# Adding the input rows on GpSimd instead of VectorE in the last stage of an attention and mixture-of-experts layer

## The reference

```python
x = x + _layernorm(_L0_attn_ref(_layernorm(x, axis=-1), ...), axis=-1)
x = x + _layernorm(_L0_ffn_ref(_layernorm(x, axis=-1), ...), axis=-1)
return x

def _L0_ffn_ref(hidden_states, ...):
    ...
    routed_sum = routed.sum(axis=0)
    shared = jax.nn.silu(x @ shared_gate_w) * (x @ shared_up_w) @ shared_down_w
    return (shared + routed_sum).reshape(orig_shape)
```

## Time and profile before

| | us |
|---|---|
| median of 3 runs | 421.2 (420.75 to 421.65) |
| the profiled execution, its time | 420.75 |
| the profiled execution, its span | 418.9 |
| PE busy in the span | 397.9 (95%) |
| DVE busy in the span | 274.7 (66%) |
| POOL busy in the span | 122.9 (29%) |

### The profile page before, as it was taken

The page is one execution under the profiler, slowest core; times in us unless marked ns, Lnnn a source line. Parts: engine busy times, 40 slices in busy tenths (PEclk is TensorE's granted clock), DMA queues, the critical chain, the costliest instruction groups (busy, mean ns, idle before and its releaser), DMA issues.

```text
span 418.9 us, 9551 instructions
## 1 busy us (share of the span) xinstructions
PE 397.9 (95%) x3443; PEld 301.6 (72%) x3443; DVE 274.7 (66%) x644; ACT 207.1 (49%) x381; POOL 122.9 (29%) x179
## 2 busy tenths in 40 slices
PE   8998999999999999898989999999999999999992
PEld 8775557676767766575768999999995444489991
DVE  5565677987879777877674694222225898736786
ACT  2745748586776757556551113444447766411110
POOL 2424514335152525303402002211222220015651
PEclk9999999999999999999999999999999999999998
DMA  8735235373634636360146750011111111114532
GB/s 259 220 109 151 64 84 189 92 228 89 217 90 123 193 87 211 101 196 1 55 140 204 246 189 27 27 50 52 52 50 39 52 40 39 40 47 120 152 113 75
DMA packets 50772, 47.29 MB, mean 113 GB/s; under 512 B 5350, under 2 KB 45542, under 8 KB 50726
## 3 DMA queue, kind: packets, MB, share of 16 engines
q1 hardware_dynamic: 44795, 38.31, 30.7%
q0 software_dynamic: 1632, 4.46, 3.7%
q10 hardware_dynamic: 4299, 3.92, 2.8%
HBM read 25.19 MB, written 8.65 MB: 81 GB/s over the span
## 4 chain that ended last, share of the span: by engine, by line
PE 81%; DVE 9%; issue 3%; ACT 3%; POOL 2%; DVEq 0%; ACTq 0%; POOLq 0%
PE bank L1420 41%; PE bank L1752 7%; PE bank L1424 6%; PE bank L1597 6%; PE bank L1617 5%; PE bank L1558 4%; PE bank L1777 3%; DVE nmax L1087 2%; PE bank L1496 2%; PE bank L1544 2%; PE bank L1433 2%; PE bank L1486 1%; DVE wall L1117 1%; DVE stats_at L991 1%; POOL rstd_at L644 1%
## 5 line engine op out<-in xcount | busy, mean ns | idle before, releaser
L1087 DVE TENSOR_REDUCE nmax<-bank 128x2 f32<-128x512 f32 x112 | 74.3, 686 | 27.3 <-PE bank L1558 26.7
L1420 PEld LDWEIGHTS bank<-stacks,wall 128*128 128x128 f32 x512 | 59.8, 192 | 2.5 <-issue 1.9
L1420 PE MATMUL bank<-stacks,wall 128*128 128x128 f32 x512 | 61.2, 276 | 0.4 <-ACT stacks L909 0.4
L1293 DVE TENSOR_TENSOR stacks<-stacks,bank 128x512 f32<-128x512 f32 x34 | 23.3, 687 | 53.3 <-PE bank L1420 50.8
L873 ACT ACTIVATE pv<-bank 128x512 f32<-128x512 f32 x64 | 38.2, 603 | 34.1 <-PE bank L1617 33.2
L909 ACT ACTIVATE stacks<-bank 128x512 f32<-128x512 f32 x34 | 20.3, 597 | 64.2 <-PE bank L1420 49.6
L873 ACT ACTIVATE wall<-bank 128x512 f32<-128x512 f32 x64 | 38.3, 606 | 24.9 <-PE bank L1617 24.8
L1617 PE MATMUL bank<-stacks 99*128 99x256 bf16 x256 | 48.8, 274 | 1.4 <-ACT wall L873 0.9
L1420 PE MATMUL bank<-wall,stacks 128*128 128x256 f32 (+1 forms) x208 | 49.2, 380 | 0.0
L1558 PE MATMUL bank<-stacks 96*128 96x256 bf16 x224 | 42.3, 273 | 4.8 <-DVE nmax L1087 4.7
L716 POOL DMA_INDIRECT stacks<-x_sc,row_i x18 | 20.3, 1125 | 89.2 <-PE bank L1424 70.1
(11 more groups left out here) (212 smaller groups left out, 795.0 us busy)
## 6 DMA issues: line engine op xcount, KB each, us to landing
stacks<-low_sb SPq DMA_DIRECT2D x144, 64.0 KB, 2.0
wall<-gate_up SPq DMA_DIRECT2D x8, 1024.0 KB, 5.5
wall<-down SPq DMA_DIRECT2D x8, 512.0 KB, 6.6
y_exp<-stacks ACTq DMA_DIRECT2D x18, 128.0 KB, 1.7
x_tok<-wall SPq DMA_DIRECT2D x8, 256.0 KB, 2.5
stacks<-x_tok SPq DMA_DIRECT2D x16, 128.0 KB
out<-stacks SPq DMA_DIRECT2D x8, 256.0 KB, 2.4
stacks<-low_sb SPq DMA_DIRECT2D x12, 128.0 KB, 2.4
```

The source lines that it names most:

```text
L1087: dve.tensor_reduce(nmax[:, half, qt, 2 * pair:2 * pair + 2], two(sm_bank[u % 2]), AX.X, ALU.max, negate=True).then_inc(sm["sm_max"], 1)
L1293: dve.tensor_tensor(to, sg, fu[:, :], ALU.mult).then_inc(sm["h_sb"], 1)
L1420: last = pe.matmul(out_ap, lhsT, rhs, start=(n == 0), stop=(n == len(pairs) - 1))
```

## The change

`plus_x` of pairs 0 to 5 leaves DVE's program and stands in POOL's, behind the power and the gather of the same `final`. It is one instruction of 128 x 512 there, where DVE had two of 128 x 256. It waits for `zn_ready` (`normalise` of that pair on DVE) and signals `fin_ready` once, so that SP's store counts c + 1 instead of 2c + 2. Pairs 6 and 7 stay on DVE. The gathers are dealt out anew: six instructions ahead of the first power (pairs 0, 1, 2), then one pair after each of the powers 0 to 4.

```diff
@@ SP
-                sp.wait_ge(*(sm["fin_last"], 2 * (c - HALF + 3)) if late else (sm["fin_ready"], 2 * c + 2))
+                sp.wait_ge(*(sm["fin_last"], 2 * (c - HALF + 3)) if late else (sm["fin_ready"], c + 1))
@@ POOL
-                for c in range(2):
+                for c in range(3):
                     gather(c)
...
-            after_power = {0: (2,), 1: (3, 4), **{c: (c + 3,) for c in range(2, HALF - 3)}}
+            after_power = {c: c + 3 for c in range(HALF - 3)}
             assert HALF == 8
+            x_two = x_sb[:, :, :].rearrange("p (g n) d -> p n g d", g=2)
 
             def final(c, n, p):
                 power("out", c + 1, rstd_f[:, p, :], var_f[:, p, :], 2)
-                for n in after_power.get(c, ()):
-                    gather(n)
+                if c in after_power:
+                    gather(after_power[c])
+                if c >= HALF - 2:
+                    return
+                plus_x(c, p)
+
+            def plus_x(c, p):
+                pool.wait_ge(sm["zn_ready"], 2 * c + 2)
+                pool.tensor_tensor(z_sb[:, p, :, :], z_sb[:, p, :, :],
+                                   x_two[:, ds(c, 1), :, :].rearrange("p a g d -> p (a g) d"), ALU.add
+                                   ).then_inc(sm["fin_ready"], 1)
@@ DVE
-            def plus_x(c):
+            def last_out(c):
+                normalise(c, c % 2)
                 dve.wait_ge(sm["zn_ready"], 2 * c + 2)
                 for g in range(2):
                     dve.tensor_tensor(z_of(c, c % 2)[:, g, :], z_of(c, c % 2)[:, g, :], x_sb[:, c + HALF * g, :], ALU.add
-                                      ).then_inc(sm["fin_last" if c >= HALF - 2 else "fin_ready"], 1)
-
-            def last_out(c):
-                normalise(c, c % 2)
-                plus_x(c)
+                                      ).then_inc(sm["fin_last"], 1)
...
                 if c != 0:
                     normalise(c - 1, 1 - p)
-                    plus_x(c - 1)
...
             def between_last():
                 normalise(HALF - 3, 1)
-                plus_x(HALF - 3)
                 first_part(HALF - 1)
```

## The result

The changed kernel takes 423.63 us (median of 6 runs, 422.99 to 424.83), the kernel before 421.01 us beside it. The ratio is 1.006, with a 95% interval of 1.0045 to 1.0075: **0.6% slower**, 2.6 us, where 0.18% less was forecast. The profiled execution took 423.33 us with a span of 421.5.

The account below looks back on a forecast made before the run. PE was taken to bound the kernel until 407.6, then DVE to the end. A 0.76 us gain at the end and 0 elsewhere gave 419.99 us for the profiled execution, 420.4 at the median; range 419.8 to 421.4.

Parts of the forecast that it names:

- So all of this costs nothing at the end: 0: Steady steps and POOL: later gathers, moved adds and late buffers are covered and add 0 to the time.
- The gathers: Ahead of power 0: two more gathers cost POOL 2 x 1.25 us, power 0 starts 0.7 late, at 382.2.
- 2.6 us of cover: Steady steps: PE loses time only if DVE comes to hidden 2.6 us late.
- a rival of 0.14: End: last down product or a semaphore comes late, so the gain is 0 to 0.4, 420.8 to 421.2 us; chance 0.14.
- POOL behind, buffers late: Steady steps: POOL's add takes 1.27 us, pair 0's store lands at 389.3, z(2) starts 0.8 late, at no cost.
- The end of the program: DVE's tail: without plus_x(5), first_part(7) starts 0.77 us earlier and the last sum at 411.16, gaining 0.76 us.
- POOL goes first: first_part(7): POOL's add of pair 5 holds DVE's L1346, 0.65 us later than before, 421.9 at the median; chance 0.06.
- POOL falls behind: Steady steps: an add over 1.9 us makes POOL's round exceed 5.30 and delay add up, 422 to 423; chance 0.04.

Follow-up runs that it names:

- the dealing alone: Kernel before with only the gathers dealt out anew (three pairs ahead of the first power), every plus_x still on DVE: 425.63 us, ratio 1.0092.
- the memset version: Changed kernel with the gathers dealt out as before and POOL's add replaced by a 128 x 1024 memset into scratch: 420.6 us, ratio 0.997.
- the kernel with this step alone: Kernel before with only plus_x of pair 5 on POOL: 420.13 us, ratio 0.9973; again with more executions 420.33 us, ratio 0.9982.
- the version with the old dealing: Changed kernel with the gathers dealt out as before, plus_x of pairs 0 to 5 still on POOL: 422.37 us, ratio 1.002.

## Why the prediction was wrong

**"So all of this costs nothing at the end: 0" was the step that failed**, in two terms. In its place the runs showed some 3.4 us: 1.8 us go with the new dealing of the gathers (2.6 with it, 0.85 without), and the held DVE instructions are worth the 0.85 us that stay plus the 0.76 that the end gained.

*The gathers.* I priced two more gathers ahead of power 0 as 2 x 1.25 us of POOL's time and found them covered. Their POOL time was right: power 0 began at 382.16, forecast 382.2. But a row of six delays PE's signal by 3.8 us, more than the 2.6 us of cover, and PE's steps shifted by 1.40 us in the changed kernel. With the dealing alone the signal was 5.3 us late, and the steps shifted by 4.5, the lower clock included. The row that should have warned was in my hands: hidden at 392.77, 1.0 us after its due time, at the end of the kernel's only other row of four. I counted it as a stray late signal and gave it a place in a rival of 0.14, without asking what POOL did at that moment. That alone would have been no proof, since two later profiles have the same row and a signal on time.

*DVE beside POOL's add.* I wrote that the trace has no case of a DVE add under a long POOL add, looked for a meeting only where the chain of waits runs, at first_part(7), and gave it 0.06. There it didn't happen. It happened in the steady steps, beside five of the six adds, and for the variance of 128 x 2 too, which costs 0.17 us by its row and over 1 us under an add. The cover of 2.6 us, right for the steady steps, is 0.9 us at the last down product, where hidden came 2.0 us late; that smaller cover was not priced either. The trace of before had a case to learn from. DVE's maxima beside POOL's wide adds (L1087) kept their length, but they read PSUM. One small instruction from SBUF to SBUF did not:

```profile
208.55 0.89 DVE L1184 TENSOR_SCALAR score<-score 128x12 f32<-128x12 f32 x1
```

POOL's add L684 runs from 208.14 to 209.41, and this instruction ends at 209.44. Two instructions later a product of two tensors of 128 x 12 takes 0.17 us. It is the held variance in small, in the rows of the kernel before.

**POOL behind, buffers late**: right in kind and right at no cost. POOL's add took 1.27 us as taken from the earlier trace rows; the waits for stores came (0.73 and 0.90 us) and the memset version shows them free.

**The end of the program**: right. first_part(7) follows normalise(5) at once, and the last sum came 0.8 us sooner behind hidden, with 0.76 forecast; the kernel with this step alone is 0.8 to 1.1 us faster. PE's last product was there about when its modelled end said (407.52 + 3.62 = 411.14): at 411.22 the last sum started without idle time.

**The rivals**: "POOL goes first" had the right mechanism at the wrong place. Its price (0.65 us over before) lies near the 0.85 us of the version with the old dealing by luck, since it was worked out for L1346 of first_part(7), which was not held. "POOL falls behind" was not needed. None of them had the gathers. The Trainium skill's rule ("SBUF — State Buffer", section "Who interferes with whom") says also that instructions in VectorE's two-port modes contend with GpSimd, that `tensor_scalar` can enter these modes, and that a two-input instruction contends with a GpSimd instruction that reads SBUF and not with one that only writes it. The held variance (1.17 us, 0.77 beside the memset) and the held normalise (1.67 us) agree with the first, the two-input adds of 0.42 us in the memset version with the last, as far as they meet a memset. Its sentence that the one which issues first goes first fits the add of pair 5, where DVE's two-input add started 0.24 us ahead and kept its 0.42. It does not fit two cases, if the starts in the trace are right. L1396 at 396.76, in the version with the old dealing, started 0.60 us ahead of POOL's add at 397.36, needs 0.42 us and yet ended 0.29 us after it, at 398.94. L1396 at 401.71 in the changed kernel started 0.61 us ahead and ended at 403.88, 0.28 us after POOL's.

**What stays open** is why a row of indirect gathers makes PE's signals late. Shown: all four profiles with six or eight in a row have it, the one with eight the most; of the seven later rows of four in the table, five have it; it moves with the row; with a pause of 2.3 us it is gone; and the same bytes from ACT's queue or as plain transfers from POOL's do no harm. Not separated is where in a row the product ends. Each late signal was due within a row or at most 0.3 us behind it, and each first row of four that did no harm ended 1.5 us ahead of the product and had no gather right behind it. So whether it takes more gathers behind the row or only a product that ends near it wasn't tried. PE itself went on with the work behind the late signal (its gate half at 382.62 is in the trace), so it is the signal and not the product that is late, if the starts in the trace are right. DVE, ACT and SP all get them late. Whether the signals of other engines are late at that time wasn't tried.

## What to carry to other kernels

An instruction moved from DVE to POOL is not gone from DVE: here POOL's add of 1.27 us held DVE's two-input adds and plain SBUF-to-SBUF instructions, in most places where they met, until it ended. So move one only to where DVE then works from PSUM or on statistics, and check each neighbour, small ones first. Price a reordering of POOL's DMAs as carefully as the move it comes with, and test it alone. And a single late signal in the profile of before is a question, not noise: look at what every other engine was doing at that moment.

## What the runs showed of the hardware that I had not expected

- Behind six indirect gathers in a row the semaphore of a finished PE product was late by 3.8 to 5.3 us, behind eight by 6.7 us, behind a later row of four by 0.8 to 1.5 us in five profiles and not at all in two; with a pause of 2.3 us behind the fourth of six it was on time.
- A DVE instruction on 2 elements in a row (the variance, 0.17 us) took up to 1.17 us beside POOL's add and 0.77 us beside a POOL memset; a two-input add of 0.42 us took up to 2.18 us beside the add and 0.42 in the version with the memset.
- After PE had stood still for 2.62 us the granted clock was 0.50 (1.2 GHz) from 388 to 390, and 16 matmuls took 3.67 us; after a stop of 1.16 us it was 1.00 and they took 2.05.
